# K's bias row added on VectorE instead of in a matmul, with another order on VectorE and in the opening

## The chip, the cores and the metric

One core of a Trainium2 chip runs the kernel. The time is the device time of one execution in microseconds; of several runs the median counts.

## What is computed

x is 16 sequences of 256 tokens with 128 features, all f32. A modulation comes from c: `mod = silu(c) @ wmod`, six rows of 128 for each sequence (shift, scale and gate of two halves).

```
h = layernorm(x) * (1 + ca) + sa
# half 1: linear attention (16 heads of 8), then layer norm, relu MLP 128-512-128, layer norm
K = elu(h @ Wk + bk) + 1 ;  Q = elu(h @ Wq + bq) + 1 ;  V = h @ Wv + bv
x = x + ga * block(h)
h = layernorm(x) * (1 + cb) + sb
# half 2: each token mixed with the one before it by mu_r, mu_k
x = x + gb * sigmoid(xr @ W_r.T) * (relu(xk @ W_k.T) ** 2 @ W_v.T)
```

The bias of K is a row: in the kernel K lies with tokens on the partitions and features along the row, so it can't be the per-partition bias of a ScalarE instruction, as Q's is (Q lies the other way round).

## The kernel before

**Tiling.** One sequence at a time; its 256 tokens are two chunks (c = 0, 1) of 128 partitions. The 16 sequences go through a software pipeline: step t works on K, Q and the state of sequence t, on the attention of t-1, on the MLP of t-2, on the middle (z, x2) of t-3, and on the token mixing of t-4. There are 17 steps and a tail written out for the last sequences. Steps 0 to 2 are written out in `first_steps` of each engine (the opening); from step 3 on `step(t)` is used.

**Order.** Each engine has its own queue in an order written out by hand, and semaphores tie them together; `need(engine, signal, count)` is such a wait. Nothing is planned at run time.

**TensorE in a step.** transposes of n1 (normalised x), attention product of t-1, transposes of ny and n3, K's product (L1203, L1206), Q's product (L1214), first MLP product (L1250), transposes of the attention, state product (L1222, waits for K's elu), output product (L1166), the mixing products with wkT (L1190, waits for the first half of mixT, `mixk_ok`) and wrT (L1194), the state's value (L1233), second MLP product (L1140) around the last product of half 2 (L1362). The end of L1140 releases z's statistics on VectorE.

**K's bias before.** The bias, less what a folded-in shift contributes, is a row in f32. It is split in the opening (`bias_part`) in three bf16 rows `bias_parts`, so that one bf16 product of ones with it (L1203, 128x256) starts K's PSUM bank (banks[4]) in every step; the two products with wk add to it. ScalarE takes the exponent out of PSUM (L333), and VectorE's `k_elu` (L836) combines it with the PSUM bank into k_sb.

**VectorE in a step.** `step_end`: statistics of z (L685), `gated` (L817), mv_z (L694). Then x's statistics of the next sequence, denominators (den, L841), mv_n of x, reciprocals (L845), `centred` (L787), `attention` (L850), `k_elu` (L836), `middle` (L797), statistics of x2 (for n3), the two mixing halves `mix_half` K_W then R_W (L822), mv_n of x2, statistics of y, `q_elu`, mv_ny, n3 (L700), `masked_state` (L858), ny (L700). In the drain (step 16) the mixing comes before `centred`. mv is mean and variance; GpSimd makes rstd out of it with a power (L534).

**ScalarE in a step.** hT (L323), x1T (L328), the kept part of the mixing (L317), exponent of K (L333), of Q, relu of Q, the MLP's relus (L347), transposed attention, state, weights, relu and square and tanh of half 2, n1 of the next sequence (L292, waits for GpSimd's shift_n1).

**Opening.** Warming matmuls (L1070) run while the loads come. VectorE and ScalarE each make one half of the first n1 (scale and shift); the modulation's products (L1076) give CA and the shift columns; hT follows.

## Time and profile before

| | us |
|---|---|
| median of 3 runs (lowest to highest) | 163.57 (163.56 to 163.71) |
| the profiled execution, its own time | 162.83 |
| its span, first to last instruction | 161.0 |
| busy: TensorE / VectorE / ScalarE / GpSimd | 156.1 / 128.8 / 116.9 / 105.1 |

The span is what the trace covers; the execution's own time is 1.83 us longer, which lies around it. The profiled execution was 0.74 us under the median. A matmul's row overlaps its neighbours' rows; what a matmul takes from the engine is the distance of the starts. Each f32 matmul shows as two rows.

### The profile page before, as it was taken

Reading aid. Unit: us, or ns where it says so; the run is one execution under the profiler, and the core shown is the slowest. Engines: PE = TensorE matmul, PEld = TensorE weight load, DVE = VectorE, ACT = ScalarE, POOL = GpSimd, SP = SyncE. Lnnn points to the kernel's source line nnn. Section 1 sums busy time; section 2 is a strip of 40 time slices with the busy share of each in tenths; the row PEclk is TensorE's granted clock in tenths of the full one; section 3 lists DMA queues with packets and bytes.
Section 4 is the critical chain, followed back from the end, with each engine's and each line's share of the span. In section 5 each row is a group of like instructions: output and inputs, shape, how many; then the busy total and the mean of one; then the engine's idle time right before and its main releaser. Section 6 shows DMA issues by size and latency. Waiting matters only on the chain.

```text
span 161.0 us, 4072 instructions
## 1 busy us (share of the span) xinstructions
PE 156.1 (97%) x1151; PEld 145.8 (91%) x1151; DVE 128.8 (80%) x585; ACT 116.9 (73%) x320; POOL 105.1 (65%) x243
## 2 busy tenths in 40 slices
PE   7999999999999999999999999999999999999992
PEld 6878898999999999999999999999999999898891
DVE  3866878698888979797988888897979878887842
ACT  4256776789695969696987959595969787556562
POOL 4337567476676767787676767676777755972631
PEclk9999999999999999999999999999999999999999
DMA  4925279940010101010100101010101000010112
GB/s 124 255 100 160 80 215 338 429 199 0 2 33 4 33 0 33 4 35 2 33 5 0 33 6 33 0 33 4 33 2 35 4 4 28 2 37 2 33 29 69
DMA packets 8973, 9.93 MB, mean 62 GB/s; under 512 B 724, under 2 KB 7416, under 8 KB 8952
## 3 DMA queue, kind: packets, MB, share of 16 engines
q1 hardware_dynamic: 8656, 9.60, 19.1%
q8 instruction: 9, 0.15, 0.4%
q10 hardware_dynamic: 296, 0.08, 0.2%
q14 instruction: 12, 0.10, 0.2%
HBM read 7.55 MB, written 2.13 MB: 60 GB/s over the span
## 4 chain that ended last, share of the span: by engine, by line
PE 88%; DVE 5%; issue 2%; POOL 2%; ACT 1%; DVEq 0%; POOLq 0%
PE bank L1140 16%; PE bank L1250 15%; PE bank L1129 8%; PE bank L1222 5%; PE bank L1206 4%; PE bank L1178 4%; PE bank L1214 4%; PE bank L1166 4%; PE bank L1134 4%; PE bank L1362 3%; PE bank L1194 3%; PE bank L1190 3%; PE bank L1233 3%; PE bank L1070 2%; PE bank L1203 1%
## 5 line engine op out<-in xcount | busy, mean ns | idle before, releaser
L1140 PE MATMUL bank<-w,hid 128*128 128x128 f32 x240 | 31.7, 275 | 0.0
L1250 PE MATMUL bank<-x1T,w 128*128 128x256 f32 x120 | 30.9, 381 | 0.0
L1140 PEld LDWEIGHTS bank<-w,hid 128*128 128x128 f32 x240 | 29.3, 192 | 0.0
L347 ACT ACTIVATE hid<-bank,b_cols 128x256 f32<-128x256 f32 x60 | 26.0, 511 | 1.1 <-PE bank L1250 1.1
L534 POOL TENSOR_TENSOR rstd_n<-vare_n,power 128x2 f32<-128x2 f32 x30 | 23.8, 792 | 2.4
L323 ACT ACTIVATE hT<-bank,modT 128x256 f32<-128x256 f32 x16 | 9.0, 564 | 20.8 <-PE bank L1129 20.7
L1250 PEld LDWEIGHTS bank<-x1T,w 128*128 128x128 f32 x120 | 21.5, 190 | 2.6 <-ACT x1T L328 0.2
L530 POOL TENSOR_TENSOR vare_n<-mv_n,eps 128x2 f32<-128x2 f32 x30 | 5.8, 194 | 17.3 <-DVE mv_n L694 17.2
L292 ACT ACTIVATE n<-x_all,shift_n,rstd_n 128x128 f32<-128x128 f32 x27 | 11.8, 485 | 2.5 <-POOL shift_n L542 2.5
L700 DVE TENSOR_SCALAR ny<-bank,mv_ny,rstd_ny 128x128 f32<-128x128 f32 x32 | 11.6, 405 | 2.5 <-POOL rstd_ny L534 1.2
L700 DVE TENSOR_SCALAR n<-x,mv_n,rstd_n 128x128 f32<-128x128 f32 x28 | 8.4, 343 | 6.0 <-POOL rstd_n L534 6.0
L317 ACT ACTIVATE keepT<-bank,modT 128x255 f32<-128x255 f32 x26 | 13.1, 555 | 0.0
L534 POOL TENSOR_TENSOR rstd_ny<-vare_ny,power 128x2 f32<-128x2 f32 x16 | 11.9, 746 | 1.3
L588 POOL TENSOR_TENSOR out_sb<-x,prod 128x256 f32<-128x256 f32 x15 | 10.9, 726 | 2.8 <-DVE x L797 1.2
L685 DVE BATCH_NORM_STATS2 stats_z<-bank 128x6 f32<-128x128 f32 x30 | 7.4, 289 | 6.0 <-PE bank L1140 5.9
L1129 PE MATMUL bank<-ident,n 128*128 128x128 f32 x62 | 11.9, 273 | 0.0
L530 POOL TENSOR_TENSOR vare_z<-mv_z,eps 128x2 f32<-128x2 f32 x14 | 2.7, 195 | 13.7 <-DVE mv_z L694 13.7
L1166 PE MATMUL bank<-kqvo,attT 128*128 128x128 f32 x64 | 11.5, 275 | 0.0
L581 POOL TENSOR_TENSOR xb<-x_all,gm_rows 128x256 f32<-128x256 f32 x15 | 10.9, 724 | 0.8 <-DVE x L797 0.8
L822 DVE SCALAR_TENSOR_TENSOR mixT<-bank,modT,keepT 128x256 f32<-128x256 f32 x26 | 11.2, 470 | 0.0
L328 ACT ACTIVATE x1T<-bank,beta_b,cols 128x256 f32<-128x256 f32 x15 | 8.5, 563 | 3.7 <-PE bank L1129 2.5
L1178 PE MATMUL bank<-kvs,qT 128*128 128x144 f32 x64 | 10.7, 289 | 0.0
(186 smaller groups left out, 454.1 us busy)
## 6 DMA issues: line engine op xcount, KB each, us to landing
gm_rows<-mod_rows_dram SPq DMA_DIRECT2D x2, 960.0 KB, 9.6
out<-out_sb SPq DMA_DIRECT2D x15, 128.0 KB, 1.8
gm_rows<-mod_rows_dram SPq DMA_DIRECT2D x1, 768.0 KB, 6.8
w<-in_w SPq DMA_DIRECT2D x1, 512.0 KB, 5.5
x_all<-in_x SPq DMA_DIRECT2D x1, 512.0 KB, 5.5
bv_row<-bv_rows_dram SPq DMA_DIRECT2D x1, 512.0 KB, 7.7
bv_row<-bv_rows_dram SPq DMA_DIRECT2D x1, 384.0 KB, 4.3
gm_rows<-mod_rows_dram SPq DMA_DIRECT2D x1, 384.0 KB, 4.1
```

Source lines behind the costliest of these rows:

```text
L292: last = nc.scalar.activation(n1[s % 2][:, c, :], x_all[:, NC * s + c, :], ACT.Identity, scale=rstd["n1"][:, c:c + 1], bias=shift_n1[:, c: ...
L317: nc.scalar.activation(keepT[:, i, 1:L], banks[2][:, 0:L - 1], ACT.Identity, scale=mod_col(KEEP + i, s), bias=mod_col(SB, s)).then_inc((ke ...
L347: last = nc.scalar.activation(hid[:, f, :], bank[:, f % 2 * L:(f % 2 + 1) * L], ACT.Relu, bias=b1_cols[:, f:f + 1])
L534: nc.gpsimd.tensor_tensor(rstd[name][:, :], vare[name][:, :], power[:, :], ALU.pow).then_inc(rstd_ok[name], 1)
L581: nc.gpsimd.tensor_tensor(tile[:, :, :], x_all[:, NC * s:NC * (s + 1), :], gm_rows[:, s, GB_ROW:GB_ROW + 1, :].broadcast_to([128, NC, D]), ...
L700: last = nc.vector.tensor_scalar(dest[:, c, :], source(c), mv[name][:, c, 0:1], rstd[name][:, c:c + 1], ALU.subtract, ALU.mult)
L822: nc.vector.scalar_tensor_tensor(mixT[:, i, :], banks[2][:, 0:L], modT[:, MOVE + i, s:s + 1], keepT[:, i, :], ALU.mult, ALU.add).then_inc( ...
L1129: last = nc.tensor.transpose(bank[:, c * 128:(c + 1) * 128], tile[:, c, :], ident[:, :])
L1140: last = nc.tensor.matmul(banks[6][:, c * D:(c + 1) * D], hid[:, f, c * 128:(c + 1) * 128], w2[:, f, :], start=False, stop=(f == FF - 1 an ...
L1166: last = nc.tensor.matmul(banks[1][:, c * D:(c + 1) * D], attT[:, c * 128:(c + 1) * 128], wo, start=False, stop=(c == NC - 1))
L1178: last = nc.tensor.matmul(attention_bank(s)[:, c * (D + H):(c + 1) * (D + H)], qT[:, c * 128:(c + 1) * 128], kvs[:, :], start=True, stop=True)
L1250: return nc.tensor.matmul(bank[:, f % 2 * L:(f % 2 + 1) * L], w1[:, f * 128:(f + 1) * 128], x1T[:, :], start=True, stop=True)
```

## The change

K's bias leaves TensorE, except for sequence 0. `bk` is loaded to all 128 partitions, and `bias_rows` is the f32 bias row on each. Only the first K product still starts with a bias product, one in f32. From sequence 1 on VectorE adds the row: `k_biased` reads the PSUM bank and writes kb in SBUF; exponent and `k_elu` read kb, and the PSUM bank is free once kb is written. VectorE's order in a step is changed: `centred` first, then denominators, reciprocals, `k_biased`, attention, x's statistics and mv_n, `k_elu`; what follows is unchanged, n3 among it. In the opening two warming matmuls and the bf16 split go; VectorE makes a first normalised n1 (mean and rstd only) in the second n1 buffer for the first transposes, ScalarE makes both halves of the real n1 of sequence 0, a separate column `shift_first` shifts the first hT, and the order of TensorE, ScalarE and VectorE in `first_steps` is another.

```diff
+        bk_rows, bias_rows = sb("bk_rows", [128, D]), sb("bias_rows", [128, D])
+        kb = sb("kb", [128, NC, D])
# ScalarE
-            act.dma_start(bias3[:, :], a["bk"]...broadcast_to([3, D])).then_inc(bias_loaded, 16)
+            act.dma_start(bk_rows[:, :], a["bk"]...broadcast_to([128, D])).then_inc(bias_loaded, 16)
             def k_exponent(s):
-                need(act, k_mm, s + 1)
-                nc.scalar.activation(exp_k[:, :, :], chunked(banks[4]), ACT.Exp, bias=neg1[:, :]).then_inc(expk_ok, 1)
+                if s == 0:
+                    act.wait_ge(k_mm, 1)
+                need(act, kb_ok, s)
+                source = kb[:, :, :] if s else chunked(banks[4])
+                nc.scalar.activation(exp_k[:, :, :], source, ACT.Exp, bias=neg1[:, :]).then_inc(expk_ok, 1)
             def first_steps():
-                h_turned(0)
+                act.wait_ge(hT_mm, 1)
+                nc.scalar.activation(hT[0][:, :], banks[0][:, 0:L], ACT.Identity, scale=mod_col(CA, 0),
+                                     bias=shift_first[:, :]).then_inc(hT_ok, 1)
+                n1_part(0, 1).then_inc(n1_ok, 1)
...
+                act.wait_ge(cols_ok, 3)
+                h_turned(1)
                 raw_columns(0)
-                h_turned(1)
                 k_exponent(1)
-                q_exponent(1)
                 raw_columns(1)
                 attention_turned(0)
+                q_exponent(1)
+                state_out(1)
                 q_relu()
-                state_out(1)
# VectorE, opening
-            nc.vector.scalar_tensor_tensor(bias_k[:, :], bias3[:, :], 1.0, banks[6][0:3, D:2 * D], ALU.add,
-                                           ALU.subtract).then_inc(parts, 1)
-            def bias_part(i):
...
+            nc.vector.scalar_tensor_tensor(bias_rows[:, :], bk_rows[:, :], 1.0, banks[6][:, D:2 * D], ALU.add,
+                                           ALU.subtract).then_inc(bias_rows_ok, 1)
-            bias_part(0)
-            n1_chunk(0, 1).then_inc(n1_half, 1)
+            normalise("n1", n1[1], x_chunk(0), 1, n1_turn)
...
+            nc.vector.tensor_tensor(shift_first[:, :], banks[1][:, 128:129], cols[:, BO:BO + 1], ALU.add).then_inc(cols_ok, 1)
...
             def k_elu(s):
                 need(dve, expk_ok, s + 1)
+                plain = kb[:, :, :] if s else chunked(banks[4])
+                nc.vector.scalar_tensor_tensor(k_sb[:, :, :], exp_k[:, :, :], 1.0, plain, ALU.min, ALU.max).then_inc(k_ok, 1)
+            def k_biased(s):
+                need(dve, k_mm, s + 1)
+                need(dve, bias_rows_ok, 1)
+                nc.vector.tensor_tensor(kb[:, :, :], chunked(banks[4]), bias_rows[:, :].unsqueeze(1).broadcast_to([128, NC, D]),
+                                        ALU.add).then_inc(kb_ok, 1)
                 x_stats(2)
                 denominators(0)
                 x_mv(2)
                 reciprocals(0)
+                k_biased(1)
                 attention(0)
+                direct_weights(1)
                 k_elu(1)
...
                 attention(1)
+                k_biased(2)
                 y_norm(0)
# VectorE, step(t)
+                if live(t):
+                    centred(sp_)
+                denominators(sb_)
+                reciprocals(sb_)
+                if live(t):
+                    k_biased(sa)
+                attention(sb_)
                 if live(t + 1):
                     x_stats(t + 1)
-                    need(dve, stats_ok["n1"], sa + 2)
-                denominators(sb_)
-                if live(t + 1):
                     need(dve, mean_ok, sa + 1)
-                    norm_mv("n1")
-                reciprocals(sb_)
-                if t == S:
-                    attention(sb_)
+                    norm_mv("n1", sa + 2)
                 if draining(t):
                     mix_half(K_W, sc)
                     mix_half(R_W, sc)
-                centred(sp_)
-                if not draining(t):
-                    attention(sb_)
-                if live(t):
+                    centred(sp_)
+                else:
                     k_elu(sa)
                 middle(sp_)
# TensorE
-            keep_warm(2)
...
             def k_product(s):
+                if s == 0:
+                    pe.wait_ge(const_dve, 6)
+                    pe.wait_ge(bias_rows_ok, 1)
+                    nc.tensor.matmul(chunked(banks[4]), ones_row[:, :], bias_rows[:, :].unsqueeze(1).broadcast_to([128, NC, D]),
+                                     start=True, stop=False)
+                elif s == 1:
+                    pe.wait_ge(k_ok, 1)
                 need(pe, hT_ok, s + 1)
-                need(pe, k_ok, s)
+                need(pe, kb_ok, s - 1)
                 need(pe, tanh_ok, s - 4)
-                nc.tensor.matmul(chunked(banks[4]), ones3[:, :], bias_parts[:, :].unsqueeze(1).broadcast_to([128, NC, D]),
-                                 start=True, stop=False)
                 for c in range(NC):
...
-                                            wk, start=False, stop=(c == NC - 1))
+                                            wk, start=(s > 0 and c == 0), stop=(c == NC - 1))
             def first_steps():
-                pe.wait_ge(n1_half, 1)
-                n1_transposes(0)
-                direct_row(0)
-                pe.wait_ge(parts, 6)
-                pe.wait_ge(const_dve, 7)
+                pe.wait_ge(n1_turn, 1)
+                transpose_in(banks[0], n1[1], hT_mm)
                 k_product(0)
                 q_product(0)
+                direct_row(0)
+                state_product(0)
                 bv_product()
-                state_product(0)
+                value_of_state(0)
+                n1_transposes(1)
+                second_modulation((2, 5), 2)
+                attention_product(0)
+
+                k_product(1)
                 pe.wait_ge(direct_ok, 1)
                 direct_row(1)
...
```

## Rows read from the trace of the kernel before

**Rows 1.** The page: busy time of each engine, and the chain that ended last.

```profile
PE 156.1 (97%) x1151; PEld 145.8 (91%) x1151; DVE 128.8 (80%) x585; ACT 116.9 (73%) x320; POOL 105.1 (65%) x243
...
PE 88%; DVE 5%; issue 2%; POOL 2%; ACT 1%; DVEq 0%; POOLq 0%
```

**Rows 2.** Timeline, step 10, TensorE: start us, duration us, engine, line, operation.

```profile
86.12 0.27 PE L1203 MATMUL bank<-bias_parts,ones 128*128 128x256 bf16 x1
...
86.23 0.61 PE L1206 MATMUL bank<-kqvo,hT 128*128 128x128 f32 x4
...
90.07 0.30 PEld L1190 LDWEIGHTS bank<-mixT,mix_w 128*128 128x128 f32 x2
...
90.18 0.60 PE L1190 MATMUL bank<-mixT,mix_w 128*128 128x256 f32 x2
```

**Rows 3.** Busy time in one step: engines with instruction counts, PEclk, DMA share, GB/s.

```profile
85.20:93.97 8.77, 8.77 (x69) 8.39 (x68) 7.54 (x35) 7.13 (x20) 6.39 (x14) 1.00 0.06 17
```

**Rows 4.** Timeline, VectorE in step 10, from z's statistics to the next ones.

```profile
85.18 0.49 DVE L685 BATCH_NORM_STATS2 stats_z<-bank 128x6 f32<-128x128 f32 x2 [0.44 <-PE bank L1140]
...
85.59 0.40 DVE L817 SCALAR_TENSOR_TENSOR prod<-tanh_r,bank 128x256 f32<-128x256 f32 x1
...
85.91 0.24 DVE L694 BATCH_NORM_AGGREGATE mv_z<-stats_z 128x2 f32<-128x6 f32 x2
...
86.07 0.45 DVE L685 BATCH_NORM_STATS2 stats_n<-x_all 128x6 f32<-128x128 f32 x2
...
86.56 0.19 DVE L841 TENSOR_SCALAR den<-bank 128x32 f32<-128x32 f32 x1
...
86.66 0.24 DVE L694 BATCH_NORM_AGGREGATE mv_n<-stats_n 128x2 f32<-128x6 f32 x2
...
86.82 0.32 DVE L845 RECIPROCAL rden<-den 128x32 f32<-128x32 f32 x1
...
87.05 0.51 DVE L787 SCALAR_TENSOR_TENSOR z<-bank,mv_z,gm_rows 128x128 f32<-128x128 f32 x2
...
87.48 0.48 DVE L850 TENSOR_TENSOR att<-bank,rden 128x128 f32<-128x128 f32 x2
...
88.07 0.42 DVE L836 SCALAR_TENSOR_TENSOR k_sb<-exp_k,bank 128x256 f32<-128x256 f32 x1
...
88.41 0.60 DVE L797 SCALAR_TENSOR_TENSOR x<-z,rstd_z,xb 128x128 f32<-128x128 f32 x2
...
89.45 0.86 DVE L822 SCALAR_TENSOR_TENSOR mixT<-bank,modT,keepT 128x256 f32<-128x256 f32 x2
...
93.95 0.49 DVE L685 BATCH_NORM_STATS2 stats_z<-bank 128x6 f32<-128x128 f32 x2 [0.44 <-PE bank L1140]
```

**Rows 5.** Timeline, ScalarE's exponent of K in step 10.

```profile
87.56 0.47 ACT L333 ACTIVATE exp_k<-bank,neg 128x256 f32<-128x256 f32 x1
```

**Rows 6.** Instructions on mixT: duration ns min/median/max, first and last start us.

```profile
L822 DVE SCALAR_TENSOR_TENSOR mixT<-bank,modT,keepT x26: 465/472/475, 36.8 to 140.2; 128x256 f32<-128x256 f32 x26
```

**Rows 7.** Timeline, step 3: ScalarE hands hT to the waiting TensorE.

```profile
25.15 0.56 ACT L323 ACTIVATE hT<-bank,modT 128x256 f32<-128x256 f32 x1 [1.02 <-PE bank L1129]
...
25.77 0.10 PEld L1203 LDWEIGHTS bank<-bias_parts,ones 128*128 128x128 bf16 x1 [0.24 <-ACT hT L323]
```

**Rows 8.** Timeline, VectorE, step 15's exponent wait and a wait for its own statistics.

```profile
131.95 0.42 DVE L836 SCALAR_TENSOR_TENSOR k_sb<-exp_k,bank 128x256 f32<-128x256 f32 x1 [0.63 <-ACT exp_k L333]
...
145.53 0.50 DVE L685 BATCH_NORM_STATS2 stats_z<-bank 128x6 f32<-128x128 f32 x2
146.13 0.25 DVE L694 BATCH_NORM_AGGREGATE mv_z<-stats_z 128x2 f32<-128x6 f32 x2
```

**Rows 9.** Timeline of the opening: warming matmuls, later y's normalisation.

```profile
4.93 1.06 PE L1070 MATMUL bank<-warm 128*128 128x128 f32 x4
...
18.17 0.72 DVE L700 TENSOR_SCALAR ny<-bank,mv_ny,rstd_ny 128x128 f32<-128x128 f32 x2
```

**Rows 10.** Busy time of the third microsecond, columns as in the other window.

```profile
2.00:3.00 1.00, 1.00 (x7) 1.00 (x7) 0.00 (x0) 0.75 (x2) 0.73 (x5) 1.00 0.92 244
```

More of the change, by code:

```diff
@@ L290, in take_n1 @@
                 wait_x(act, s)
[L291 to L293 removed]
+                for c in range(NC):
+                    last = n1_part(s, c)
                 last.then_inc(n1_ok, 1)
[L296 removed]
+            act.wait_ge(x_in[0], 16)
+            act.wait_ge(shift_n1_ok, 1)
+            n1_part(0, 0)
             act.wait_ge(cols_ok, 2)
@@ L1191, in mix_products @@
                     need(pe, mix_ok, sc + 1)
[L1192 removed]
+                    need(pe, kb_ok, sc + 4, LAST)
                     for c in range(NC):
```

65 lines of the change are left out of this document (19 added, 46 removed).

## The prediction

> **What bounds the kernel now.** I read the page first. TensorE is busy for 156.1 of 161.0 us, VectorE for 128.8, ScalarE for 116.9, GpSimd for 105.1, and the chain that ended last lies on TensorE for 88% of the span [rows 1]. The reader should see there an engine without room, and a second one, VectorE, with little.
>
> A busy row says nothing about stalls of matmuls that overlap, so I took one steady step (step 10) and went through its timeline. Two starts of z's statistics on VectorE, 85.18 and 93.95, give the period: 8.77 us [rows 4]. TensorE is busy for all 8.77 of it [rows 3]. K's bias product starts at 86.12 and the product behind it at 86.23, although its own row says 0.27: what it takes from TensorE is the difference of the starts, 0.11 us [rows 2]. This is the price of the thing that the change removes.
>
> Then I looked for the wait that comes nearest to ending last. The product with wkT (L1190) needs the first half of mixT. VectorE starts the two halves at 89.45 [rows 4]; one half takes 0.472 [rows 6]; so the first is there at 89.92. A waiting TensorE starts 0.06 behind the end of what releases it: hT ends at 25.15 + 0.56 = 25.71, the weight load starts at 25.77 [rows 7]. So L1190's weight load could have started at 89.98, and it did at 90.07 [rows 2]. The slack is 0.09 us, in a step of 8.77. Seen as a loop: z's statistics to the first half of mixT 4.27, the half 0.47, the wake 0.06, and from the weight load at 90.07 to the next statistics at 93.95 another 3.88; that is 8.68, against TensorE's 8.77. The kernel is bound by TensorE, and a loop through VectorE is only 0.09 behind it. Where K's elu stands in this loop VectorE also waits for ScalarE: the attention pair starts at 87.48, and behind such a pair (0.48 long, with 0.08 of overlap as in the pair of statistics, 0.49 long and 0.41 to the next start) K's elu could start at 87.88; it starts at 88.07, 0.04 after the exponent's end at 88.03 [rows 4, 5]. So 0.19 of idle time lies there. Step 15, which has no x statistics to take, shows this wait larger, 0.63 [rows 8].
>
> **The change in a steady step, TensorE.** The bias product goes: -0.11 a step. The rest of TensorE's order stays. Only if nothing else is late does this count.
>
> **The change in a steady step, VectorE.** In front of the mixing, one instruction is added (k_biased, 128x256 out of PSUM plus a row) and the order is new. I lay the new order out from the start of z's statistics, with the starts of rows 4: gated at 0.41, mv_z at 0.73, ending 0.97. `centred` now follows at once and waits for mv_z on its own engine: 0.04 (x's statistics end at 86.52, den starts at 86.56), so 1.01; before, x's statistics hid this. den 0.43 later, 1.44; the reciprocal waits for den, 0.19 + 0.04, so 1.67; before, mv_n hid this. k_biased after 0.23, the reciprocal's distance to the next start, so 1.90. k_biased itself: the trace has none; nearest is K's elu, which reads the same 256 elements of PSUM and one SBUF tile and is followed 0.34 later (88.07 to 88.41). Bounds are 0.20, half of the attention pair, and 0.47, a mixing half. I take 0.34, since shape and operands are the same. attention at 2.24; x's statistics 0.40 later, 2.64; mv_n directly behind them must wait for their end, 0.45, and 0.10 more, as mv_z waits behind its own statistics (145.53 + 0.50, start 146.13 [rows 8]): 3.19. K's elu 0.16 later: 3.35. Before it was 88.07 - 85.18 = 2.89. **VectorE reaches K's elu, and so the mixing, 0.46 us later.** Of the 0.34 for k_biased and the lost covers (0.08 at mv_z and den, mv_n's own 0.16 that used to lie under den's wait, and the waits), 0.19 has been paid back by the idle time at the exponent.
>
> The exponent is not what is late: k_biased ends at 1.90 + 0.42 = 2.32, ScalarE is woken at 2.38, which is the 87.56 of before [rows 5], and ends at 2.85, well ahead of 3.35.
>
> **Where it goes.** The loop through the mixing is 4.27 + 0.46 + 0.47 + 0.06 + 3.88 = 9.14 us. TensorE alone would need 8.66. So the loop sets the period: +0.37 a step (0.46 less the slack of 0.09), and the 0.11 given back by the bias product becomes idle time of TensorE in front of L1190. K's elu is also what the state product waits for; this is the same 0.46 ahead of the same L1190, and not added. Behind the mixing VectorE hands on its lateness to n3, y and the GpSimd powers, and in front of the next z statistics it was idle for 0.44 [rows 4]; with a period 0.37 longer it has 0.81 of room for 0.46, so this side stays covered. GpSimd gets x's moments later (mv_n at 3.19 instead of 86.66 - 85.18 = 1.48), but its next work on n3 comes later too; it is busy for 6.39 of 8.77 [rows 3].
>
> If the cover were complete (VectorE's additions under 0.09), the same edits would bring -0.11.
>
> **Which steps.** The mixing runs in steps 4 to 15. Steps 4 to 14 have the order above: 11 x 0.37 = +4.07. Step 15 takes no x statistics: K's elu waited 0.63 for the exponent there [rows 8], which holds the new instruction, so VectorE is not later, and TensorE gains what its slack allows, -0.09. Step 3 has no mixing: I set it to nothing, between -0.11 (the bias product) and +0.2 (ScalarE's queue behind the exponent starts later by about half of k_biased). Step 16 has the same order on VectorE as before, and so has the end.
>
> **The opening.** Gone are two warming matmuls, four rows from 4.93 that last 1.06 [rows 9], and the split of the bias in two bf16 parts. The first transposes now need only the mean and rstd, and K's first product has its bias (one f32 product, so two rows, shown nowhere at this place) in the shadow of hT. So everything up to step 1 can be up to 1.06 earlier. But VectorE's queue now has k_biased(2) between attention(1) and y's first normalisation at 18.17 [rows 9], which the first feed-forward product waits for; and k_biased(1) stands in front of attention(0). Each takes 0.34 out of it. I take -0.15, near nothing, because two such insertions stand against a gain of perhaps 0.8; bounds -1.0 and +0.3. bk now goes to 128 partitions: 64 KB at the 244 GB/s of that stretch [rows 10] is 0.26 us of the loads; that is the +0.3.
>
> **Sum.** 4.07 - 0.09 + 0 - 0.15 = +3.8 us. The profiled execution took 162.83 us with a span of 161.0, the median is 163.57, 0.74 more; the difference carries over: 163.6 + 3.8 = **167.4 us**, with a span near 164.8.
>
> A rule on VectorE's starts is weighed here. The rows show that k_biased's neighbour, K's elu, is 0.42 long and followed after 0.34 [rows 4]. The Trainium skill, "VectorE: DVE Perf Modes", section "The DRAIN you can't avoid", says that "the next op does not start until the 8-stage pipe empties"; read by that, k_biased would cost its whole duration. The trace does not agree for instructions without a wait between them. By the rule the sum would be the one of the third rival.
>
> **Rivals.**
> 1. *TensorE stays the bound* (the other side). For it: it is 97% busy, VectorE 80%, and there is 0.44 of idle time on VectorE at the end of each step. Against it: this idle time lies behind the mixing, not before it. It decides from the point where VectorE's additions ahead of the mixing, net of the freed wait, fall under 0.09 a step; my bounds leave 0.18 at the least. Then 13 steps x -0.11 (3 to 15) and -0.15: 162.0 us.
> 2. *The opening is late*: bias_rows stands in VectorE's queue in front of the first normalisation, and waits for a 64 KB load among loads at 0.92 of the DMA's time [rows 10]. The opening then is +0.3 instead of -0.15: 167.8 us.
> 3. *Each instruction holds the next one for its whole duration*, 0.42 instead of 0.34: 11 x 0.08 more, 168.3 us. Against it stand the starts of rows 4.
> 4. *Small steps, large opening*: k_biased at 0.20, both own-engine waits hidden, so +0.18 - 0.09 = +0.09 a step, 1.0 in all, and the opening gives its whole 1.0: about 163.5 us, no change.
>
> **How the numbers follow.** The forecast 0.67; rival 1 0.13; rival 2 0.07; rival 3 0.07; rival 4 0.06. A measurement of this kernel tells some 0.2% (0.3 us) from no change. Faster 0.13, same 0.06, slower 0.81. Steps: the low bound (+0.09 each, +0.8 in all with the other terms) gives 164.4; the high one (k_biased 0.47, the wait behind mv_z 0.10 instead of 0.04: +0.19 a step) gives 11 x 0.56 and 169.5. The range 164.0 to 169.0 leaves out rival 1 (0.13), half of rival 4 and the extreme of the steps (0.03 each).
>
> **What would show it.** Right: z's statistics 9.1 apart in steps 4 to 14, TensorE idle for some 0.4 in front of L1190, released by mixT; K's elu 3.3 to 3.4 after z's statistics. In step 15 no such stall. If the period is 8.66 or so, the loop argument is wrong. If it lies between, a start to start distance is mis-sized; the same rows tell which. If TensorE idles elsewhere (at the state product, at y's transposes), my choice of the last wait is wrong. The start of the first feed-forward product shows the opening.

## The result, and the profile after

The kernel after took 170.03 us (median of 4 runs, 169.46 to 170.25), the kernel before 163.56 beside it (4 runs, 162.94 to 163.71): ratio 1.0397, 95% interval 1.0361 to 1.0434. It is 6.5 us slower; the forecast was 3.8 us slower, and its range ended at 169.0. The profiled execution took 170.25 us with a span of 168.3.

The page after, answering to [rows 1]: busy time, then the chain that ended last.

```profile
PE 161.2 (96%) x1133; PEld 145.7 (87%) x1133; DVE 134.9 (80%) x595; ACT 118.9 (71%) x321; POOL 106.2 (63%) x243
...
PE 56%; DVE 30%; issue 8%; DMA 2%; ACT 1%; POOL 1%; DVEq 0%; SPq 0%; POOLq 0%
```

TensorE's share of busy time is unchanged in effect (97 to 96%), but the chain went from 88% on TensorE to 56%, with 30% on VectorE: a loop now runs through two engines. The busy row alone would have hidden this.

Starts of z's statistics on VectorE cut the difference of the spans into parts (they are read off the timeline, step by step):

| stretch | before | after | difference | forecast |
|---|---|---|---|---|
| to step 3 | 24.87 | 26.65 | +1.78 | -0.15 |
| step 3 | 7.87 | 7.90 | +0.03 | 0 |
| steps 4 to 14 | 96.32 | 101.97 | +5.65 | +4.07 |
| step 15 | 8.78 | 8.85 | +0.07 | -0.09 |
| rest of the span | 23.2 | 22.9 | -0.2 | 0 |

Two terms are off: the steady step is +0.51 where +0.37 was forecast, and the opening is late by 1.8.

**The steady step.** Step 10 on VectorE after, answering to [rows 4]; the first row and the last are a period apart, 9.29.

```profile
90.10 0.50 DVE L692 BATCH_NORM_STATS2 stats_z<-bank 128x6 f32<-128x128 f32 x2 [0.43 <-PE bank L1139]
90.52 0.40 DVE L810 SCALAR_TENSOR_TENSOR prod<-tanh_r,bank 128x256 f32<-128x256 f32 x1
90.84 0.24 DVE L701 BATCH_NORM_AGGREGATE mv_z<-stats_z 128x2 f32<-128x6 f32 x2
91.11 0.61 DVE L780 SCALAR_TENSOR_TENSOR z<-bank,mv_z,gm_rows 128x128 f32<-128x128 f32 x2
91.64 0.18 DVE L840 TENSOR_SCALAR den<-bank 128x32 f32<-128x32 f32 x1
91.85 0.35 DVE L844 RECIPROCAL rden<-den 128x32 f32<-128x32 f32 x1
92.12 0.36 DVE L835 TENSOR_TENSOR kb<-bank,bias_rows 128x256 f32<-128x256 f32 x1
92.40 0.48 DVE L849 TENSOR_TENSOR att<-bank,rden 128x128 f32<-128x128 f32 x2
92.80 0.48 DVE L692 BATCH_NORM_STATS2 stats_n<-x_all 128x6 f32<-128x128 f32 x2
93.40 0.25 DVE L701 BATCH_NORM_AGGREGATE mv_n<-stats_n 128x2 f32<-128x6 f32 x2
93.57 0.39 DVE L830 SCALAR_TENSOR_TENSOR k_sb<-exp_k,kb 128x256 f32<-128x256 f32 x1
...
94.92 0.86 DVE L815 SCALAR_TENSOR_TENSOR mixT<-bank,modT,keepT 128x256 f32<-128x256 f32 x2
...
99.39 0.30 DVE L692 BATCH_NORM_STATS2 stats_z<-bank 128x6 f32<-128x128 f32 x1 [0.43 <-PE bank L1139]
```

The same stretch on TensorE after, answering to [rows 2] (PEld is the weight load), and under it its waits over the whole span: waiter, what it waited for, us in all, times, longest.

```profile
91.05 0.66 PE L1210 MATMUL bank<-kqvo,hT 128*128 128x128 f32 x4
91.55 0.60 PE L1218 MATMUL bank<-hT,kqvo 128*128 128x256 f32 x2
...
94.01 0.52 PEld L1226 LDWEIGHTS bank<-k_sb,n 128*128 128x128 f32 x4 [0.32 <-DVE k_sb L830]
...
95.51 0.30 PEld L1189 LDWEIGHTS bank<-mixT,mix_w 128*128 128x128 f32 x2 [0.31 <-issue]
```

```profile
PEld bank L1226 <- DVE k_sb L830: 3.9, 13, 0.3
...
PEld bank L1189 <- issue: 3.4, 11, 0.3
```

Mixing starts 4.82 behind z's statistics (before 4.27, forecast 4.73); its first half takes 0.47, so it ends at 95.39; the weight load starts at 95.51, 0.12 later, where the forecast had 0.06; from there to the next statistics it is 3.88, as before. 4.82 + 0.47 + 0.12 + 3.88 = 9.29. TensorE idles in front of L1189 eleven times, in steps 4 to 14 and only there. The profile calls the releaser "issue"; that it is mixT is read from the times, and e7 and e11 below show it. The wait for K's elu at L1226 is part of the same lateness: in e2 below, with the same order on VectorE, the state product waits for it in only five places (1.1 us in all), and the mixing's weight load still waits in eleven (3.1 us).

**The opening.** TensorE's first rows after (before, the first product with kqvo started at 3.92, the first of the feed-forward at 20.04), and the DMA issues in the first 12 us: KB each, median us from issue to landing.

```profile
3.19 0.85 PE L1070 MATMUL bank<-warm 128*128 128x128 f32 x3
4.91 0.80 PE L1082 MATMUL bank<-cols,kqvo 128*128 128x128 f32 x2 [0.87 <-DMA kqvo<-in_kqvo]
...
5.92 1.06 PE L1076 MATMUL bank<-siluT,wmod 128*128 128x128 f32 x4
...
8.56 1.23 PE L1210 MATMUL bank<-kqvo,hT 128*128 128x128 f32 x4
...
10.80 0.71 PE L1226 MATMUL bank<-k_sb,n 128*128 128x128 f32 x4
...
22.03 0.81 PE L1254 MATMUL bank<-x1T,w 128*128 128x256 f32 x3
```

```profile
kqvo<-in_kqvo SPq DMA_DIRECT2D x2, 128.0 KB, 3.5
...
bk_rows<-in_bk ACTq DMA_DIRECT2D x1, 64.0 KB, 3.7
```

kqvo (Wk and Wq among them) took 2.9 from issue to landing before, 3.5 now, and TensorE has nothing to do until it is there. The windows from 3 to 4 us, before and then after, show that the loads did not merely have more to carry (last three columns: granted clock, DMA share, GB/s):

```profile
3.00:4.00 1.00, 1.00 (x6) 0.82 (x5) 0.49 (x2) 0.22 (x1) 0.00 (x0) 1.00 0.88 237
```

```profile
3.00:4.00 1.00, 1.00 (x5) 0.74 (x4) 0.69 (x5) 0.21 (x1) 0.00 (x0) 1.00 0.63 148
```

With the 64 KB load among them the loads together move less in this microsecond, not more; in the next one they move 301 GB/s and before 213, so it is a delay and not a lasting loss of rate.

### The profile page after: what moved, and what is told of

Read it like the earlier page. It is cut to its first block, busy times and chain, and to the rows that moved or that the text cites. A ratio compares the mean times of both kernels' runs of the same rounds, so it can differ in the third digit from the quotient of the medians.

```text
span 168.3 us, 4064 instructions
## 1 busy us (share of the span) xinstructions
PE 161.2 (96%) x1133; PEld 145.7 (87%) x1133; DVE 134.9 (80%) x595; ACT 118.9 (71%) x321; POOL 106.2 (63%) x243
## 4 chain that ended last, share of the span: by engine, by line
PE 56%; DVE 30%; issue 8%; DMA 2%; ACT 1%; POOL 1%; DVEq 0%; SPq 0%; POOLq 0%
PE bank L1139 15%; DVE stats_n L692 6%; PE bank L1189 5%; PE bank L1254 4%; DVE z L780 4%; DVE x L790 4%; PE bank L1364 3%; PE bank L1193 3%; PE bank L1133 3%; DVE att L849 3%; DVE mixT L815 3%; DVE kb L835 3%; PE bank L1128 2%; PE bank L1237 2%; DVE stats_z L692 2%
## 5 line engine op out<-in xcount | busy, mean ns | idle before, releaser
L351 ACT ACTIVATE hid<-bank,b_cols 128x256 f32<-128x256 f32 x60 | 25.3, 488 | 1.2 <-PE bank L1254 1.2
L324 ACT ACTIVATE hT<-bank,modT 128x256 f32<-128x256 f32 x15 | 8.5, 564 | 20.3 <-PE bank L1128 20.3
L538 POOL TENSOR_TENSOR vare_n<-mv_n,eps 128x2 f32<-128x2 f32 x30 | 6.9, 230 | 23.1 <-DVE mv_n L701 22.9
L284 ACT ACTIVATE n<-x_all,shift_n,rstd_n 128x128 f32<-128x128 f32 x28 | 12.3, 487 | 2.6 <-POOL shift_n L550 2.6
L1226 PEld LDWEIGHTS bank<-k_sb,n 128*128 128x128 f32 x64 | 8.5, 190 | 4.2 <-DVE k_sb L830 3.9
L1226 PE MATMUL bank<-k_sb,n 128*128 128x128 f32 x64 | 11.1, 297 | 0.0
```

What stands on the lines that cost most here:

```text
L284: return nc.scalar.activation(n1[s % 2][:, c, :], x_all[:, NC * s + c, :], ACT.Identity, scale=rstd["n1"][:, c:c + 1], bias=shift_n1[:, c: ...
L351: last = nc.scalar.activation(hid[:, f, :], bank[:, f % 2 * L:(f % 2 + 1) * L], ACT.Relu, bias=b1_cols[:, f:f + 1])
L1226: last = nc.tensor.matmul(banks[3][:, 0:D], n1[s % 2][:, c, :], k_sb[:, c, :], start=(c == 0), stop=(c == NC - 1))
```

## The experiments

"Before" and "after" are the two kernels; ratios are to the kernel before, run on the same chip at the same time (its medians there: 162.92 for e1 to e4, 163.21 for e5 to e8, 162.92 for e9 to e12, 163.67 for e13 to e16). Period is the median of steps 5 to 14, T3 the start of step 3's z statistics, both from the profiled execution.

| run | edit to | us | ratio [95%] | period | T3 |
|---|---|---|---|---|---|
| before | | 163.57 | 1 | 8.78 | 24.87 |
| after | | 170.03 | 1.0397 [1.0361, 1.0434] | 9.28 | 26.65 |
| e1 | before | 164.77 | 1.0078 [1.0042, 1.0115] | 8.78 | 26.46 |
| e2 | before | 167.15 | 1.0267 [1.0220, 1.0315] | 9.13 | 25.16 |
| e3 | after | 165.42 | 1.0135 [1.0097, 1.0172] | 8.90 | 26.01 |
| e4 | after | 171.19 | 1.0506 [1.0470, 1.0541] | 9.28 | 27.65 |
| e5 | after | 169.25 | 1.0372 [1.0346, 1.0397] | 9.28 | 25.70 |
| e6 | after | 173.62 | 1.0633 [1.0591, 1.0676] | 9.61 | 26.05 |
| e7 | after | 165.70 | 1.0148 [1.0113, 1.0183] | 8.96 | 26.17 |
| e8 | after | 164.71 | 1.0092 [1.0064, 1.0120] | 8.88 | 25.09 |
| e9 | after | 169.20 | 1.0372 [1.0346, 1.0398] | 9.28 | 25.48 |
| e10 | before | 163.01 | 1.0004 [0.9989, 1.0019] | 8.78 | 24.83 |
| e11 | after | 168.44 | 1.0334 [1.0290, 1.0377] | 9.22 | 26.20 |
| e12 | before | 163.24 | 1.0009 [0.9989, 1.0028] | 8.81 | 25.03 |
| e13 | before | 162.55 | 0.9944 [0.9923, 0.9966] | 8.71 | 24.97 |
| e14 | after | 169.27 | 1.0351 [1.0312, 1.0390] | 9.29 | 25.45 |
| e15 | e12 | 162.47 | 0.9934 [0.9908, 0.9960] | 8.71 | 25.04 |
| e16 | before | 163.27 | 0.9977 [0.9956, 0.9999] | 8.77 | 24.85 |

Where an experiment leaves the opening of the kernel after as it is (e3, e6, e7, e11), T3 lies between 26.0 and 26.2; the 26.65 of the kernel after is at the late end of what this opening does. Differences under half a microsecond in T3 say little.

The us of a run hold more than its span, and that part isn't steady: in the 21 executions of the kernel before beside e13 to e16 it is 1.8 to 3.3 us (median 2.6), beside the other groups 1.9 to 2.0 in the median, in e13, e15 and e16 1.7 to 1.9. So where a ratio lies within 1% of 1 the spans are compared as well.

### One part at a time: e1, e2, e3

e1, the load alone:

```diff
-        bias3 = sb("bias3", [3, D])
+        bias3 = sb("bias3", [128, D])
-            act.dma_start(bias3[:, :], ....broadcast_to([3, D]))
+            act.dma_start(bias3[:, :], ....broadcast_to([128, D]))
```

> The kernel before, with one edit: bk is loaded to 128 partitions (64 KB) instead of 3; the rest reads rows 0 to 2 of it. Theory L (the opening's loss is the load): the first load of Wk and Wq is late by about 1 us and TensorE, idle meanwhile, takes longer over what follows, so the first feed-forward product moves from 20.0 to 21.0 to 22.0 and the time rises by 1.0 to 2.0 us. Rival O (the loss comes from the new orders and the missing warming matmuls): within 0.3 us of before.

Besides this only the instruction that reads bias3 is narrowed to its rows 0 to 2, and the opening is late by the load: in e1's timeline TensorE waits for kqvo as it does in the kernel after.

```profile
4.88 0.80 PE L1082 MATMUL bank<-cols,kqvo 128*128 128x128 f32 x2 [0.85 <-DMA kqvo<-in_kqvo]
```

T3 is 1.59 later, the period the same. The loss is not in every execution: of the ten (163.09 to 165.71 us), three have spans of 161.1 to 161.3, as the kernel before, and seven 162.4 to 163.2. That this depends on how the loads interleave is a guess; the trace shows one of the late ones. The four spans of the kernel after, 167.7 to 168.3, have no such early group.

e2, the new order on VectorE without the addition, K's bias product kept:

```diff
+                if live(t):
+                    centred(sp_)
                 denominators(sb_)
                 reciprocals(sb_)
                 attention(sb_)
                 if live(t + 1):
                     x_stats(t + 1)
                     need(dve, mean_ok, sa + 1)
                     norm_mv("n1", sa + 2)
...
                     k_elu(sa)
```

> The kernel before, with VectorE's new order in the steps and nothing else: the bias product stays on TensorE and there is no k_biased. Theory V (the loop through the mixing sets the period, and the order pays for two own-engine waits and mv_n): K's elu about 3.19 and the mixing about 4.55 after z's statistics (2.89 and 4.27 before), period 9.02 instead of 8.78, +2.7 us over 11 steps. Rival K (the loss is the added instruction, order is neutral): period 8.78, same time.

The order alone makes the period 0.35 longer. K's elu stands 3.32 behind z's statistics, the mixing 4.67 (before 2.89 and 4.27), and 4.67 + 0.47 + 0.12 + 3.88 gives 9.14, where 9.13 is measured.

e3, the addition in the old order (the fence shows it against the order of the kernel before):

```diff
                 reciprocals(sb_)
+                if live(t):
+                    k_biased(sa)
...
                 centred(sp_)
                 attention(sb_)
                 if live(t):
                     k_elu(sa)
```

> The changed kernel, with VectorE's steps in the order of before and k_biased behind the reciprocals. Theory V: mixing about 4.38 after z's statistics, loop 4.38 + 0.47 + 0.12 + 3.88 = 8.85, so about 0.44 less a step than the changed kernel's 9.29, -4.8 us, near 165.2. Rival K (the added instruction is the loss): as the changed kernel less at most 0.1 a step, near 169.

With the old order the addition costs 0.13 a step: K's elu is at 3.06, the mixing at 4.44. So of the steady loss about 0.35 is the order and 0.13 the addition (together 0.48 of 0.51). The name of the change points at the smaller part. The way of the 0.13 is not only the one expected. The sum through the mixing, 4.44 + 0.47 + 0.12 + 3.88 = 8.91, fits the period, but TensorE's idle time lies elsewhere, in front of the third product of the feed-forward, whose bank z must have left; the addition stands in front of `centred` here and makes z late:

```profile
PEld bank L1257 <- DVE z L780: 3.4, 11, 0.4
```

Both limits lie close together: e8 below, which takes the mixing out of the way and keeps this wait, gains only 0.02.

### The loop through the mixing: e6, e7, e10, e11

e6, the addition done twice in steps 4 and later (the first result goes nowhere):

```diff
+                if s > 3:
+                    nc.vector.tensor_tensor(kb2[:, :, :], chunked(banks[4]), bias_rows[...], ALU.add)
                 nc.vector.tensor_tensor(kb[:, :, :], chunked(banks[4]), bias_rows[...], ALU.add).then_inc(kb_ok, 1)
```

> The changed kernel with k_biased's addition done twice in steps 4 to 15 (the first time into a tile that nobody reads). Theory V: each step's mixing is later by one more start to start distance of this instruction, 0.28: period 9.57 instead of 9.28, +3.1 us over steps 4 to 14, nothing more than about 0.1 in step 15. Rival (something other than VectorE's queue sets the period): less than half of this.

The period is 0.33 longer, the mixing 0.33 later (5.15): what is put ahead of the mixing is paid in full, at the distance of the starts. Its VectorE rows:

```profile
93.49 0.36 DVE L837 TENSOR_TENSOR kb<-bank,bias_rows 128x256 f32<-128x256 f32 x1
93.77 0.41 DVE L839 TENSOR_TENSOR kb<-bank,bias_rows 128x256 f32<-128x256 f32 x1
94.10 0.48 DVE L853 TENSOR_TENSOR att<-bank,rden 128x128 f32<-128x128 f32 x2
```

The one behind the reciprocal is followed after 0.28, its twin after 0.33.

e7, the two mixing halves of the kernel after ahead of `middle`; e10, the same edit to the kernel before (there the mixing starts 3.23 behind z's statistics):

```diff
+                if live(t - 4) and not draining(t):
+                    mix_half(K_W, sc)
+                    mix_half(R_W, sc)
                 middle(sp_)
...
                 norm_stats("n3", lambda c: x2_p[:, c, :])
-                if live(t - 4) and not draining(t):
-                    mix_half(K_W, sc)
-                    mix_half(R_W, sc)
```

> The changed kernel with the two mixing halves moved in front of the middle (directly behind K's elu). Theory V: the mixing no longer ends last; the state product, which waits for K's elu (3.47 + 0.39 + 0.05 = 3.91 behind z's statistics, where TensorE could take it at 3.56), does: 0.11 of restart, 1.22 to the mixing product and 3.88 on give a period near 9.0, 0.3 to 0.4 less a step, so 3 to 4 us faster than the changed kernel. Rival (the middle's chain, x2 to n3 to GpSimd's power, is what is late): no gain, or slower.

> The kernel before with the mixing halves ahead of the middle. If TensorE bounds the kernel before, as the prediction has it, the time is the same within 0.3 us (163.2), period 8.78. If the loop through the mixing sets it already, the period falls by up to 0.1 to 0.3 and the time by 1 to 3 us.

One move of two instructions takes 0.32 a step off the kernel after and nothing off the kernel before, where the mixing comes 1.04 earlier and the period stays 8.78. So the loop through the mixing bounds after, and TensorE bounds before. With the mixing out of the way e7's bound is K's elu, as its waits show:

```profile
PEld bank L1226 <- DVE k_sb L830: 4.8, 14, 0.4
```

e11, one wait fewer in front of the mixing products of the kernel after (the dropped one is implied by other waits):

```diff
-                    need(pe, attT_ok, sc + 4)
                     need(pe, mixk_ok, sc + 1)
```

> The kernel after without the second, redundant wait in front of the mixing products. If the 0.12 us from the end of the mixing half to the weight load is the price of two waits, it falls to 0.06: period 9.22, the time 0.7 us shorter (169.3). If it is the latency of the wake itself, nothing changes (170.0).

```profile
94.12 0.86 DVE L815 SCALAR_TENSOR_TENSOR mixT<-bank,modT,keepT 128x256 f32<-128x256 f32 x2
```

```profile
94.64 0.30 PEld L1188 LDWEIGHTS bank<-mixT,mix_w 128*128 128x128 f32 x2 [0.25 <-DVE mixT L815]
```

The half ends at 94.12 + 0.47 = 94.59, the weight load starts at 94.64: 0.05 instead of 0.12, and the releaser is now called by its name. It isn't the bare number of waits that costs this: the state product at L1226 stands behind three, and starts 0.05 behind K's elu (93.57 + 0.39 = 93.96, start 94.01 in the kernel after), but there the one that comes last is the first in the queue. In front of L1189 the one that comes last, for mixT, is the second. That the place in the queue decides is read from these rows; no run exchanges two waits. The period falls by 0.06 or 0.07. The 1.6 us between the medians of e11 and after is more than the 0.7 of such steps; in the profiled executions 0.45 of it lies in the opening (T3).

### The opening: e4, e5, e9, e14

e4, the load issued behind the tanh, bias_rows computed behind the first normalisation:

```diff
-            act.dma_start(bk_rows[:, :], ...)
             nc.scalar.activation(tanh_c[:, :], cols[:, 0:S], ACT.Tanh, scale=0.5).then_inc(tanh_c_ok, 1)
+            act.dma_start(bk_rows[:, :], ...)
```

> The changed kernel, with bk's load to 128 partitions issued behind ScalarE's tanh (near 3.3 us instead of 1.3) and, on VectorE, the bias row computed behind the first normalisation. Theory L: Wk and Wq land near 3.9 again instead of 4.85, TensorE has no 0.87 of idle time there, and the opening is 1.0 to 2.0 us shorter; the steps keep their period of 9.29. Rival O: no change beyond 0.3 us.

A miss. kqvo comes on time (its first product at 3.83), but the row, issued 1.7 us later (3.06 instead of 1.33), lands some 4.8 us after its issue, and the first K product waits for it longer than was won:

```profile
8.31 0.82 PE L1202 MATMUL bank<-bias_rows,ones_row 128*128 128x256 f32 x2 [1.90 <-DVE bias_rows L735]
```

Behind this wait TensorE also gets a lower clock. In the windows of a microsecond from 8 on the granted clock (third column from the end) falls from 1.00 to 0.50, its 1.2 GHz level, stays there until 12 and is back at 13; in the other runs it is 1.00 in each of these windows:

```profile
8.00:9.00 1.00, 0.69 (x3) 0.33 (x3) 0.97 (x8) 0.65 (x2) 0.00 (x0) 0.85 0.94 360
9.00:10.00 1.00, 1.00 (x6) 1.00 (x6) 0.45 (x4) 0.30 (x1) 0.26 (x2) 0.50 0.44 169
...
12.00:13.00 1.00, 1.00 (x9) 0.64 (x8) 1.00 (x4) 0.28 (x1) 0.00 (x0) 0.94 0.00 0
```

So e4 doesn't price the late row alone.

e5, two warming matmuls more:

```diff
-WARM = 6
+WARM = 8
```

> The changed kernel with 8 warming matmuls at the start instead of 6, so that TensorE is busy until about 5.0, when Wk and Wq have landed, instead of idle from 4.04 to 4.91. Theory P (part of the opening's loss is that, behind this idle time, TensorE goes on at the slow spacing of its rows, 0.21 us each, until 9.9): the spacing changes to 0.11 at 6 to 7, the first feed-forward product is 0.5 to 0.9 earlier than 22.0, the time falls by as much. Rival (only the late landing counts): within 0.2 us.

TensorE then is not idle before kqvo's first product (4.72), the first feed-forward product starts at 21.07 instead of 22.03, and T3 is 0.95 earlier than in the kernel after. Against e3, e6, e7 and e11, which have the idle time too, it is only 0.3 to 0.5 earlier, so the gain is between these values; the spans are 167.2 to 167.7 against 167.7 to 168.3. The idle time alone is not what makes the rows slow. In each of these openings the f32 rows (of 128 columns) are 0.21 us or more apart from the first one on, and at some point the distance falls to 0.11: near 6.0 in the kernel before, near 7.2 in e9 below (neither has the idle time), near 8.3 to 8.9 in e3, e6, e7 and e11, at 9.9 in the kernel after. In these runs the granted clock reads 1.00, its 2.4 GHz level, all the while, though in e4 the rows are just as far apart where it reads 0.50. What sets the point is not shown; in e5 the rows are 0.11 to 0.12 apart from 6.5 on:

```profile
5.74 0.88 PE L1076 MATMUL bank<-siluT,wmod 128*128 128x128 f32 x4
6.45 0.39 PE L1070 MATMUL bank<-warm 128*128 128x128 f32 x2
```

e9, bk as one row and a product more that spreads it:

```diff
-            act.dma_start(bk_rows[:, :], a["bk"]....broadcast_to([128, D]))
+            act.dma_start(bk_rows[0:1, :], a["bk"]...)
+            nc.tensor.matmul(banks[6][:, D:2 * D], neg_row[:, :], bk_rows[:, :], start=True, stop=False)
             nc.tensor.matmul(banks[6][:, D:2 * D], cols[...].broadcast_to([128, 128]), wk, start=False, stop=True)
```

> The kernel after, with bk loaded as one row (0.5 KB) and spread over the partitions by one more f32 product, so that the 64 KB load is gone from the opening; the steady step is untouched. Theory L (the big load delays kqvo, and what follows): TensorE's L1082 starts near 3.8 as before, step 3's z statistics near 25.1 (after 26.65), the time 1.5 us under the kernel after: 168.5. Theory O (the opening is late because of its new order): the start of step 3 stays near 26.6 and the time at 170.0. Both: steady period 9.28.

kqvo is in time, and 1.17 of the 1.78 is gone (0.5 to 0.7 against the T3 of e3, e6, e7 and e11); the spans, 167.1 to 167.4, are 0.9 under those of the kernel after. The remaining 0.6 shows late in the opening, where the kernel before started the output product at 19.23 (e9, TensorE):

```profile
3.82 0.63 PE L1087 MATMUL bank<-cols,kqvo 128*128 128x128 f32 x2
...
19.59 0.44 PE L1136 MATMUL bank<-ident,ny 128*128 128x128 f32 x2 [0.19 <-DVE ny L714]
...
20.13 0.14 PEld L1141 LDWEIGHTS bank<-ident,hT 128*128 128x128 f32 x1 [0.34 <-ACT attT L315]
```

Both waits lie behind the addition of sequence 2, which stands in front of y's normalisation and holds K's exponent on ScalarE, behind which the transposed attention queues. e14 moves both:

```diff
                 attention(1)
+                y_norm(0)
                 k_biased(2)
-                y_norm(0)
...
+                attention_turned(1)
                 k_exponent(2)
                 q_exponent(2)
-                attention_turned(1)
```

> e9 with the addition of sequence 2 behind y's first normalisation on VectorE, and the transposed attention of sequence 1 ahead of K's exponent of sequence 2 on ScalarE. If this addition in front of y's normalisation is what still makes the opening late, the first feed-forward product starts 0.5 to 0.7 earlier than in e9 (20.85), near 20.2, and the time is 0.6 us under e9 (168.6). If something ahead of it is late, nothing changes.

A miss in size. The output product moves to 19.18, 0.95 earlier, but the feed-forward behind it only 0.26, since the x1T that it reads hardly moves on ScalarE (19.99, in e9 20.07); the exponent and the others now stand between:

```profile
20.59 1.59 PEld L1262 LDWEIGHTS bank<-x1T,w 128*128 128x128 f32 x8 [0.72 <-ACT x1T L332]
```

T3 and the time stay. So moving one insertion there exposes the next, and which instruction sets T3 in e9 is open.

### What the addition costs where nothing hides it, and a version that hides it: e8, e12, e13, e15, e16

e8 puts together e3's order, e7's move and e9's row (the fence shows the steps against the order of the kernel before):

```diff
                 reciprocals(sb_)
+                k_biased(sa)
                 centred(sp_)
                 attention(sb_)
                 k_elu(sa)
+                mix_half(K_W, sc)
+                mix_half(R_W, sc)
                 middle(sp_)
```

> What the runs so far point to, together: k_biased in the order of before (behind the reciprocals), the mixing halves in front of the middle, and bk loaded as one row (0.5 KB) and spread over the partitions by one f32 product that adds into the bias product's bank. Theories V and L: period 8.67, TensorE's own, in steps 4 to 15 (0.11 less than before, -1.3 us in 12 steps), Wk and Wq at 3.9; near 161.5 us, 1% under before. If the load isn't what made the opening late, near 163.2.

A miss: 8.88. The addition in front of `centred` makes z late, and the third product of the feed-forward waits for it (its bank is z's), as in e3:

```profile
PEld bank L1265 <- DVE z L785: 3.5, 11, 0.5
```

e12 keeps the opening of the kernel before, loads the 128 rows behind the mixing weights, adds on VectorE only from sequence 3 on, and orders VectorE anew:

```diff
+            sp.dma_start(bk_rows[:, :], a["bk"]....broadcast_to([128, D])).then_inc(bkr_loaded, 16)
...
+                    denominators(sb_)
+                    reciprocals(sb_)
+                    centred(sp_)
+                    k_biased(sa)
+                    attention(sb_)
+                    x_stats(t + 1)
+                    k_elu(sa)
+                    norm_mv("n1", sa + 2)
+                    mix_half(K_W, sc)
+                    mix_half(R_W, sc)
+                middle(sp_)
```

> The opening of before, bk on 128 partitions loaded behind the mixing weights, the addition on VectorE only from sequence 3 on, and an order on VectorE in which the mixing halves come ahead of the middle and x's statistics cover waits. If the loss lies in the loop through the mixing and in the opening, and in nothing else, TensorE without its bias product is the bound again: period 8.67, start of step 3 as before (24.9), 13 x -0.11 = -1.4, 161.8 us. If the move to VectorE has a price of its own wherever it stands (ScalarE later, the PSUM bank held longer), the period stays at 8.8 or above and the time at 163.5 or more.

Neither: the opening is as before to 0.16, but the period is 8.81 and the span 0.5 longer (161.5 against 161.0 in the median). In its rows on TensorE and, last, ScalarE

```profile
86.45 0.66 PE L1225 MATMUL bank<-kqvo,hT 128*128 128x128 f32 x4
86.95 0.60 PE L1233 MATMUL bank<-hT,kqvo 128*128 128x256 f32 x2
...
89.12 0.63 PEld L1241 LDWEIGHTS bank<-k_sb,n 128*128 128x128 f32 x4
89.81 0.14 PEld L1149 LDWEIGHTS bank<-ident,hT 128*128 128x128 f32 x1
...
89.35 0.41 ACT L314 ACTIVATE attT<-bank 128x256 f32<-128x256 f32 x1
```

K's product takes 0.50 to the next start. With the bias product ahead of it, it took 0.45, from 86.23 [rows 2] to Q's product in the kernel before:

```profile
86.68 0.60 PE L1214 MATMUL bank<-hT,kqvo 128*128 128x256 f32 x2
```

So without the bias product TensorE gains 0.11 - 0.05 = 0.06. And L1149 starts 0.05 behind the end of the transposed attention on ScalarE (89.35 + 0.41 = 89.76), where ScalarE's exponent now takes 0.51 instead of 0.47 [rows 5] and everything behind it is 0.04 later.

e13 takes the bias product away and adds nothing (K has no bias from sequence 3 on), with the mixing early and the transposed attention ahead of the first relu on ScalarE; e16 is that ScalarE move alone, in the kernel before; e15 is e12 with this move and e11's:

```diff
# e13, e15, e16, ScalarE
+                attention_turned(sb_)
                 hidden_out(sd, 0)
-                attention_turned(sb_)
# e13, TensorE
+                if s < 3:
                     nc.tensor.matmul(chunked(banks[4]), ones3[:, :], bias_parts[...], start=True, stop=False)
```

> The kernel before without K's bias product from sequence 3 on (K has no bias there: that part is left out of the computation), the mixing halves ahead of the middle and the transposed attention ahead of the first relu on ScalarE, so that nothing but TensorE should bound it. By the prediction's term the product costs 0.11 a step: period 8.66, 13 steps, 1.4 us under before (161.5). By the rows of e12 (K's product takes 0.50 to the next start instead of 0.45) it is 0.06 a step: period 8.71, 0.8 us under before (162.1).

> The control: the kernel before with the transposed attention ahead of the first relu on ScalarE. TensorE bounds it, so the same period, 8.78, and the same time as before within 0.3 us. If ScalarE's order were a gain of its own, the period would fall here too.

> e12 with the transposed attention ahead of the first relu on ScalarE, and without the redundant wait in front of the mixing products. If e12's missing gain lies in TensorE's wait for the transposed attention, the period falls from 8.80 to 8.71 and the time to 0.8 us under before (162.1). If the addition on VectorE has another price, the period stays above 8.75.

e13: period 8.71, so the bias product costs TensorE 0.06 a step and not 0.11, and no more than this can be won by taking it away. e16: 8.77, so ScalarE's order gives the period nothing by itself; it has a price in steps 3 and 4, which take 16.96 together and before 16.42, with a wait of 0.58 for a_sb at the state's value in step 3 (before 0.21). So by its spans e16 is not quite what was expected, the same as before: they are 161.4 to 161.8, those of the kernel before 160.8 to 161.4. e15: 8.71 as well, with the whole addition on VectorE. In its rows the same L1149, 4.31 behind z's statistics in e12, stands at 4.16 (z's statistics start at 85.31) and no longer waits:

```profile
89.47 0.14 PEld L1149 LDWEIGHTS bank<-ident,hT 128*128 128x128 f32 x1
```

e15's ratio to the kernel before is 0.9934 (0.9908 to 0.9960), which would be 1.1 us. Most of this is not the kernel's work: the median of its spans is 160.7 and that of the kernel before 161.0, so 0.3 us, 0.2%, lies inside the span, and the rest is the larger time outside it of the kernel before. In the trace, steps 5 to 15 bring 0.72; T3 (0.17), step 3 (0.12) and step 4 (0.16), where the order of ScalarE costs, give 0.45 of it back. The ratios of e13 and e16 hold the same share from outside the span. So what is shown is that the addition can be hidden on VectorE without loss, and a gain of 0.3 us. Against the kernel after e15's span is 7.4 us shorter (160.7 against 168.1, 4.4%).

## Why the prediction was right in direction and too small

Two terms failed. The opening was forecast at -0.15 and came out at +1.78, because the 64 KB load was priced by its own bytes and not by what it delays. The steady step was forecast at +0.37 and came out at +0.51, because `centred` to den took 0.53 instead of 0.43, and TensorE's load started 0.12 instead of 0.06 behind the half; both had been read at places with other neighbours. The bound after the change, the loop through the mixing, was right.

**The bound, before.** Right. e10 moves the mixing 1.04 earlier and nothing happens.

**The loop through the mixing.** Right as a mechanism: 11 waits in front of L1189 in steps 4 to 14, none in step 15, period = mixing + half + wake + 3.88, and e6 and e7 move the period with the mixing. The steady step failed in size, +0.51 instead of +0.37, that is 1.58 us over 11 steps. Its terms, as distances of starts:

| term | forecast | measured |
|---|---|---|
| mv_z to `centred` | 0.28 | 0.27 |
| `centred` to den | 0.43 | 0.53 |
| den to reciprocal | 0.23 | 0.21 |
| reciprocal to k_biased | 0.23 | 0.27 |
| k_biased to attention | 0.34 | 0.28 |
| x's statistics to mv_n | 0.55 | 0.60 |
| mv_n to K's elu | 0.16 | 0.17 |
| K's elu to the mixing | 1.38 | 1.35 |
| end of the half to TensorE's load | 0.06 | 0.12 |

The largest error is `centred`: [rows 4] show its pair directly behind the reciprocal, 0.51 long; in every run where something else stands in front of it (after, e3, e6) it is 0.61. I took the distance from a place that the change took away. Along the chain on VectorE the errors partly cancel, +0.20 against -0.12, which is luck. k_biased came out cheaper for the same reason, since it now stands behind the reciprocal. The wake of 0.06 was read from L1203 in step 3, which stands behind two waits as well, but with the one that comes last, for hT, in front; e11 gives the other 0.06 back. With 0.12 for it the slack of the kernel before was also 0.03 and not 0.09 (89.92 + 0.12 = 90.04, start 90.07).

**The exponent.** Right for steps 4 to 14: it starts 2.42 behind z's statistics and ends well before K's elu.

```profile
92.52 0.51 ACT L337 ACTIVATE exp_k<-kb,neg 128x256 f32<-128x256 f32 x1
```

But it is 0.51 long out of kb instead of 0.47 out of PSUM, which the forecast left out; it costs nothing in after. In e12 it puts the transposed attention 0.04 later, and TensorE then waits for that.

**Step 15.** Forecast -0.09, measured +0.07. K's elu waits 0.18 there and not 0.63, but it starts at 2.96 instead of 2.89 and the mixing follows. The -0.09 also rested on the 0.11 of the bias product.

**The bias product's 0.11.** Wrong in size: 0.06 (e13). Rival 1 would have been 13 x 0.06 at the most and not 13 x 0.11. It hid behind the loop and cost the forecast nothing, but it is the measure of what this edit could bring.

**The opening.** The term that failed most: -0.15, with +0.3 as its bound, measured +1.78. The load was priced by its bytes, 64 KB at 244 GB/s. e1's trace shows 1.59 for this load alone, though three of its ten executions lose nothing, and the way is not the one of rival 2 (VectorE waiting for the row) but kqvo's landing a microsecond later. TensorE's rows also stay at double distance longer, which e5 shortens; why is open. e9, without the load, takes 1.17 off. The two insertions, in front of y's normalisation and of the attention, were counted at 0.34 each against a gain of 0.8; e9 leaves 0.6 for the new order as a whole, and e14 doesn't settle which instruction it is.

**The drain.** A rule on VectorE's starts had been weighed as a rival. k_biased is followed after 0.28 at a length of 0.36, in e6 its twin after 0.33 at 0.41. The Trainium skill, "VectorE: DVE Perf Modes", section "The DRAIN you can't avoid", would have the next one start only when the pipe is empty. Read as the whole recorded duration, as I did, that sentence does not agree with these rows; they agree with the section's addition that a next op that is not held starts earlier. The +0.9 us that I had worked out from the rule is no part of the difference.

**Sum.** Opening +1.93 more than forecast, steady steps +1.58, step 15 +0.16, step 3 +0.03, rest -0.2: 3.5, which is the span's +7.3 less the forecast's 3.8. The profiled executions differ by 7.4 and the medians by 6.5, because the profiled one of the kernel before was 0.7 under its median and that of the kernel after 0.2 over.

## What to carry to other kernels

When work moves from the engine that bounds to another one, ask first where the receiving engine next hands something back, and count every start between there and the receiving instruction; a reorder that comes with the move can cost more than the moved instruction (0.35 against 0.13 here). Take a start-to-start distance only from a place with the same neighbours, above all for what stands behind a reciprocal or behind several waits. Price a small load by what it delays among the loads around it, not by its bytes. And when a gain is under 1%, compare the spans too: here the time outside them moved by more than the kernel did.

## What the runs showed of the hardware

- A load of one 512-byte row to 128 partitions (64 KB) among the opening's loads made the 128 KB load of kqvo land in 3.5 instead of 2.9 us, and the core's loads ran at 148 instead of 237 GB/s between 3 and 4 us (after against before). Issued 1.7 us later it took 4.8 us itself (e4).
- A TensorE weight load whose last wait stood second started 0.12 behind its release (after, L1189), with that wait alone 0.05 (e11), and with it as the first of three also 0.05 (after, L1226).
- The pair of `centred` is 0.51 long directly behind the reciprocal and 0.61 elsewhere, the addition 0.36 and 0.41. e12 has both in the other constellation, and both lengths swap.
- K's f32 product needs 0.50 to the next start by itself (e12) and 0.45 behind the bf16 bias product (before).
- TensorE's f32 rows in the opening were 0.21 to 0.25 us apart until 6.0 us in the kernel before, 7.2 in e9 and 9.9 in the kernel after, and 0.11 apart behind that, with the granted clock at 1.00 all along. Why is open.
- Behind 1.9 us of waiting TensorE's granted clock read 0.85 between 8 and 9 us, 0.50 between 9 and 12, and 0.94 between 12 and 13 (e4).
